# Wider entries in the token table of a routed expert layer: 64 bytes instead of 8, with the table filled later

## The reference, cut to what matters

```
x = x + tanh(g_xattn) * attention(layernorm(x), ctx, ctx)     # 8 heads, over the features
xt = layernorm(x).reshape(-1, 512)                             # 2048 tokens
probs = softmax(xt @ wg)                                       # 8 experts
idx = argmax(probs); gate = probs[idx]
out = gate * (xt @ W[idx].T + b[idx])                          # only the chosen expert counts
x = x + tanh(g_ffn) * out
```

## Time and profile before

| | us |
|---|---|
| three runs, median (lowest to highest) | 635.13 (632.38 to 635.82) |
| the profiled execution's own time | 634.65 |
| its span, first to last instruction | 633.0 |
| PE busy | 534.4 |
| DVE busy | 451.8 |
| POOL busy | 370.9 |
| ACT busy | 349.5 |

### The profile page before, as it was taken

The page is one execution under the profiler, slowest core; times in us unless marked ns, Lnnn a source line. Parts: engine busy times, 40 slices in busy tenths (PEclk is TensorE's granted clock), DMA queues, the critical chain, the costliest instruction groups (busy, mean ns, idle before and its releaser), DMA issues.

```text
span 633.0 us, 9589 instructions
## 1 busy us (share of the span) xinstructions
PE 534.4 (84%) x2603; PEld 181.2 (29%) x2603; DVE 451.8 (71%) x883; ACT 349.5 (55%) x429; POOL 370.9 (59%) x631
## 2 busy tenths in 40 slices
PE   0177999999999999999889999998699699199993
PEld 0011222323323233232223233232222145045551
DVE  5587799889898898989988898889686545001110
ACT  2221768677787777878657777865467521011110
POOL 6434458867675776768575777857253733424441
PEclk9999999999999999999989999999999799689997
DMA  4755375766667577665454657574720433323410
GB/s 128 200 141 175 71 185 137 194 164 194 181 185 220 157 186 181 181 181 131 127 152 101 156 140 136 135 128 96 67 86 1 153 130 118 111 82 108 130 52 0
DMA packets 35045, 85.52 MB, mean 135 GB/s; under 512 B 10232, under 2 KB 10364, under 8 KB 34976
## 3 DMA queue, kind: packets, MB, share of 16 engines
q1 hardware_dynamic: 22848, 59.46, 39.1%
q0 software_dynamic: 12160, 25.62, 12.2%
HBM read 62.56 MB, written 27.15 MB: 142 GB/s over the span
## 4 chain that ended last, share of the span: by engine, by line
PE 44%; DVE 29%; DMA 8%; issue 7%; ACT 4%; POOL 4%; SPq 1%; another core or an unknown queue 1%; POOLq 0%; ACTq 0%; DVEq 0%
DVE neg_max L801 21%; PE ps_scores L1223 11%; PE ps_pv L1166 11%; PE ps_ring L1129 11%; PE ps_scores L1147 6%; ACT probs L726 3%; DMA prep<-k_perm 2%; DMA table_dram<-entries,dest_i 1%; DMA stacks<-shift_parts 1%; DVE den_turned L827 1%; PE ps_scores L1206 1%; PE ps_pv L1175 1%; POOL prep L472 1%; PE ps_pv L1183 1%; DMA recs<-recs_dram,token_cols 1%
## 5 line engine op out<-in xcount | busy, mean ns | idle before, releaser
L801 DVE TENSOR_REDUCE neg_max<-ps_ring 128x1 f32<-128x512 f32 x512 | 333.3, 682 | 58.6 <-PE ps_ring L1129 51.4
L726 ACT ACTIVATE probs<-ps_scores 128x1024 f32<-128x1024 f32 x256 | 250.2, 1022 | 94.5 <-PE ps_scores L1147 86.7
L1129 PE MATMUL ps_ring<-stacks 96*128 96x512 bf16 x512 | 199.9, 404 | 58.9 <-DMA stacks<-parts_dram 29.5
L1147 PE MATMUL ps_scores<-stacks 128*128 128x512 bf16 x512 | 155.9, 387 | 9.4 <-ACT probs L726 5.5
L1166 PE MATMUL ps_pv<-probs,v_ones 128*32 128x512 f32 x1024 | 138.6, 614 | 0.0
L1129 PEld LDWEIGHTS ps_ring<-stacks 96*128 96x128 bf16 x512 | 49.5, 97 | 251.5 <-DVE neg_max L801 201.7
L1223 PE MATMUL ps_scores<-w_sb,f_xt 128*128 x184 | 84.9, 605 | 0.9 <-ACT f_xt L719 0.9
L1147 PEld LDWEIGHTS ps_scores<-stacks 128*128 128x128 bf16 x512 | 48.1, 101 | 54.6 <-ACT probs L726 18.2
L519 POOL DMA_DIRECT2D stacks<-shift_parts x96 | 49.6, 520 | 20.3 <-POOL shift_parts L512 17.5
L719 ACT COPY f_xt<-ps_scores 128x512 f32<-128x512 f32 x23 | 13.4, 587 | 86.5 <-PE ps_scores L1206 86.5
L1223 PEld LDWEIGHTS ps_scores<-w_sb,f_xt 128*128 128x128 f32 x184 | 35.6, 195 | 37.2 <-issue 36.3
(11 more groups left out here) (139 smaller groups left out, 481.1 us busy)
## 6 DMA issues: line engine op xcount, KB each, us to landing
parts_dram<-prep POOLq DMA_DIRECT2D x16, 768.0 KB
stacks<-parts_dram SPq DMA_DIRECT2D x64, 192.0 KB
stacks<-parts_dram SPq DMA_DIRECT2D x64, 128.0 KB
w_sb<-w_t SPq DMA_DIRECT2D x16, 512.0 KB, 8.7
recs_dram<-rec SPq DMA_DIRECT2D x16, 512.0 KB, 11.4
prep<-x_perm SPq DMA_DIRECT2D x16, 256.0 KB, 5.0
prep<-k_perm SPq DMA_DIRECT2D x16, 256.0 KB, 8.7
v_in<-v_t SPq DMA_DIRECT2D x16, 256.0 KB, 9.9
```

The source lines that it names most:

```text
L726: nc.scalar.activation(probs[:, k % 2, 2 * jp:2 * jp + 2], ps_scores[:, jp], ACT.Exp).then_inc(exp_done, 1)
L801: nc.vector.tensor_reduce(neg_max[:, g, j, c:c + 1], ps_ring[:, u.slot(n)], AX.X, ALU.max, negate=True).then_inc(ring_free, 1)
L1129: nc.tensor.matmul(ps_ring[:, u.slot(n + c)], q_stack[0:KS, B.p, g, j, c * 128:(c + 1) * 128], k_stack[0:KS, B.p, g, j], start=True, stop= ...
L1147: last = nc.tensor.matmul(ps_scores[:, jp, j % 2], k_stack[0:KA, B.p, g, j, c * 128:(c + 1) * 128], q_stack[0:KA, B.p, g, j], start=True, ...
```

## The change: entries of 16 int32, and a later, larger fill

An entry becomes WIDE = 16 int32 (64 bytes), of which the first two are used as before. `table_dram` grows from 16384 * 8 bytes (128 KB) to 16384 * 64 bytes (1 MB), `entries` from 128 bytes to 1 KB and `slot_tokens` from 256 bytes to 2 KB in each partition; a block of 32 entries is 2 KB instead of 256 bytes. The fill moves from SP's list before the rounds to the end of `emit` of batch 1, behind `load_values` of batch 3, and reads each row of `none_i` eight times. POOL gets a fifteenth constant that clears all of `entries`, its first setting of `slot_tokens` is eight times as long, and the later ones set the token numbers alone.

```diff
--- before.py
+++ after.py
@@ -37,6 +37,7 @@
 
 
 TILE, ENTRY = 128, 32
+WIDE = 16
 NSLOT = NT // TILE + NE - 1
 
 
@@ -139,7 +140,7 @@
 
         parts_dram = nc.dram_tensor("parts_dram", [NB, 2, NP, ROWS, DM], BF16, kind="Internal").ap()
         recs_dram = nc.dram_tensor("recs_dram", [NT, REC], F32, kind="Internal").ap()
-        table_dram = nc.dram_tensor("table_dram", [NE * CAP, 2], I32, kind="Internal").ap()
+        table_dram = nc.dram_tensor("table_dram", [NE * CAP, WIDE], I32, kind="Internal").ap()
         table_blocks = table_dram.rearrange("(k p) o -> k (p o)", p=ENTRY)
 
 
@@ -209,7 +210,7 @@
         place = sb("place", [128, NB, NE])
         dest_f = sb("dest_f", [128, NB])
         dest_i = sb("dest_i", [128, NB], I32)
-        entries = sb("entries", [128, NB, 2], I32)
+        entries = sb("entries", [128, NB, WIDE], I32)
         count = sb("count", [128, NE])
 
         recs = sb("recs", [128, NREC, REC])
@@ -230,7 +231,7 @@
         expert_cols = sb("expert_cols", [128, 32])
         slot_expert = sb("slot_expert", [128, len(PHASES), 32], I32)
         choose_bias = sb("choose_bias", [128, len(PHASES), 32], BF16)
-        slot_tokens = sb("slot_tokens", [128, 32, 2], I32)
+        slot_tokens = sb("slot_tokens", [128, ENTRY, WIDE], I32)
         token_cols = sb("token_cols", [128, len(PHASES), 32], I32)
         gate_cols = sb("gate_cols", [128, len(PHASES), 32])
 
@@ -286,7 +287,7 @@
         STACK_CONSTS, VALUE_CONSTS = 2, 3
         DVE_CONSTS = 20
         BIAS_CLEAR = VALUE_CONSTS + 7
-        POOL_CONSTS = 14
+        POOL_CONSTS = 15
         block = ctx.enter_context(nc.Block())
 
         start_turns = Turns(0)
@@ -380,8 +381,6 @@
             load_rows_keys(Batch(1, 0))
             for g in range(NG):
                 load_stack(Batch(0, 1), g)
-            sp.wait_ge(pool_const, POOL_CONSTS)
-            sp.dma_start(table_dram.rearrange("(k p) o -> k (p o)", p=128), none_i[:]).then_inc(table_set, 16)
             sp.wait_ge(dve_const, BIAS_CLEAR)
             for j in range(3):
                 sp.dma_start(bias_rows[32 * j:32 * j + NE], bias.rearrange("(e n) -> e n", e=NE)).then_inc(bias_in, 16)
@@ -402,6 +401,10 @@
                 if stack:
                     load_stack(B.plus(2), 1)
                     load_values(B.plus(2))
+                if B.known(1):
+                    sp.wait_ge(pool_const, POOL_CONSTS)
+                    sp.dma_start(table_dram.rearrange("(k h p) o -> k h (p o)", h=WIDE // 2, p=256 // WIDE),
+                                 none_i[:].unsqueeze(1).to_broadcast([128, WIDE // 2, 256])).then_inc(table_set, 16)
 
             rounds(sp, emit)
             store_record(Batch(7, 0))
@@ -427,8 +430,10 @@
                                             allow_small_or_imprecise_dtypes=True),
                      lambda: nc.gpsimd.iota(slot_iota[:], [[0, 1]], base=0, channel_multiplier=1,
                                             allow_small_or_imprecise_dtypes=True),
+                     lambda: nc.gpsimd.iota(entries[:].rearrange("p b o -> p (b o)"), [[0, NB * WIDE]], base=0,
+                                            channel_multiplier=0),
                      lambda: nc.gpsimd.iota(entries[:, :, 0], [[ROWS, NB]], base=0, channel_multiplier=1),
-                     lambda: nc.gpsimd.iota(slot_tokens[:].rearrange("p q o -> p (q o)"), [[0, 64]], base=NONE,
+                     lambda: nc.gpsimd.iota(slot_tokens[:].rearrange("p q o -> p (q o)"), [[0, ENTRY * WIDE]], base=NONE,
                                             channel_multiplier=0),
                      lambda: nc.gpsimd.iota(count[:], [[CAP, NE]], base=0, channel_multiplier=0,
                                             allow_small_or_imprecise_dtypes=True)]
@@ -541,8 +546,7 @@
                 pool.wait_ge(table_out, 16 * GROUPS[PHASES[phase][0]][1])
                 if phase > 0:
                     pool.wait_ge(cols_ready, phase)
-                    chain.add(nc.gpsimd.iota(slot_tokens[:].rearrange("p q o -> p (q o)"), [[0, 64]], base=NONE,
-                                             channel_multiplier=0))
+                    chain.add(nc.gpsimd.iota(slot_tokens[:, :, 0], [[0, ENTRY]], base=NONE, channel_multiplier=0))
                     chain.settle()
                 pool.indirect_dma_start(slot_tokens[:].rearrange("p q o -> p (q o)"), None, table_blocks,
                                         bass.IndirectOffsetOnAxis(ap=slot_block[:, 0:1], axis=0),
```

## The result

Seven runs of the changed kernel gave a median of 630.1 us (628.8 to 631.65), seven of the kernel before 635.82 us (632.38 to 637.71). The ratio is 0.9914, with an interval from 0.9889 to 0.9939: the change makes the kernel faster by 0.6 to 1.1%. The profiled execution after took 630.53 us, 628.9 of them in the span, 4.1 less than the 633.0 before. Two executions far outside the others, one of 890.85 us in d1 and one of 1762.04 us in f1, are left out of the medians further down.

The account below looks back on a forecast made before the run. It took the chain as mostly PE and DVE, transfers counting only where an engine on it waits. Terms 0 - 0.2 + 0 + 0 + 0.35 - 0.05 = +0.1 us gave 635.2 us, range 632.3 to 638.3.

Parts of the forecast that it names:

- The scatters: 16 table scatters on POOL, each moving 8 KB instead of 1, said to be off the path: 0 us.
- The faster one: Rival: the old fill held up the stretch after 40 us; PE's whole 2.49 us wait goes, 632.9 us; chance 0.08.
- The term of the old fill: Removing the fill before the rounds shortens PE's wait ahead of batch 0's scores: gain of 0.2 us, between 0 and 2.49.
- The new fill: 1 MB fill on SP's queue at about 114 us, taking 3.0 us, hidden by idle engines and later room: 0 us.
- the rival of a dear fill: The moved fill is dear per packet, 7.0 us, and stalls batch 3 by 4.0 us: 639.2 us; chance 0.10.
- POOL's constants: Longer clearing and first setting at POOL's start, 0.78 us, covered by 0.91 us of idle time: 0 us.
- The reads: Table reads: the earlier ones hidden; the last, on the chain, +0.35 us (0 to 1.94), its clearing 0.05 off.
- The third rival: Wide blocks slow at the end: last read of 4.4 us and doubled transposes, 1.94 + 0.45, so 637.2 us; chance 0.08.

Follow-up runs that it names:

- d1: The changed kernel plus twelve extra scatters of packed 8-byte entries to an unread scratch tensor, at the places of the kernel before: 636.77 us, ratio 1.0017.
- f1: The kernel before with an unread 8 KB tensor declared behind the table and filled once: 635.71 us, ratio 1.0013.
- e6: The kernel before, 8-byte entries and early fill, with 128 more entries per expert, so regions 17,408 bytes apart: 628.03 us, ratio 0.9894.
- f3: The kernel before without the scatters of batches 0 to 11: 627.25 us, but only the stretch ahead of 480 us is to be compared.
- f4: The kernel before with scatters of batches 0 to 11 sent by token number into one stretch: 629.35 us, only ahead of 480 us to be compared.
- a2: The changed kernel measured once more, unaltered: 629.42 us, ratio 0.9911.
- e2: The changed kernel with its 1 MB fill back in the old place before the rounds, so the width alone: 629.14 us, ratio 0.9909.
- e1: The changed kernel with entries of 8 bytes, so the moved fill alone: 637.02 us, ratio 1.0016.
- e3: The changed kernel, entries still 64 bytes apart, but scattering only the first 8 bytes of each: 629.67 us, ratio 0.9908.
- e4: The changed kernel with entries of 32 bytes: 630.45 us, ratio 0.9902.
- e5: The changed kernel with entries of 16 bytes, so regions 32,768 bytes apart: 629.35 us, ratio 0.9903.
- e7: The changed kernel with the weights of batch 0 loaded in batch 8: 627.67 us, ratio 0.9892.
- f6: The same kernel as e7, measured again: 630.15 us, ratio 0.9921.
- f5: The kernel before with the edits of e6 and e7 together: 627.93 us, ratio 0.9891.
- f2: The kernel before, 8-byte entries, with 4096 entries per expert, so regions 32,768 bytes apart: 628.73 us, ratio 0.9898.

## Why the prediction was wrong

- **The scatters: the step that failed.** "No gain, then, and no cost." The prediction asked who waits for a scatter's landing, found nobody, and stopped. It did not ask what a scatter does to other transfers. Shown by e6, f3 and f4: the eight groups of 8-byte entries 16,384 bytes apart hold up shift rows, values and record stores in batches 12 to 14, from some 4 us to 9 for the shift rows, even when they are issued 10 us behind the last scatter (442.2 and 451.9 us), and with that goes a batch 14 whose first half is 4.7 us longer. The worth was some 5.6 us of the rounds. The premise behind it, that a transfer counts only where an engine on the chain waits for it, missed a transfer that slows others.
- **It was to be seen in the trace of before.** The prediction compared shift rows with their reader in batches 2 and 15 alone, 5.0 to 5.4 us and 1.6 us. In batch 12 they took 9.4, in batch 14 8.4; a half batch took 18.29 us where 13.6 was possible; ACT stood 5.42 us without a named releaser; and 1% of the chain was "an unknown queue". None of this names the scatters, but they lie there.
- **None of the rivals had it.** The faster one was at the start, and went the other way: PE's wait there did not fall from 2.49 us but rose to 3.96 (3.17 in a2). Its first scores came at 59.44 us, not within 0.5 of 57.4. The term of the old fill, -0.2, had the wrong sign: the wait is 2.09 to 2.72 us in the profiles with the early fill (before, e2, e6, f1 to f4) and 3.07 to 3.96 with the moved one (after, a2, e1, e3, e4, e5). At the fourth turn the first seven stand at 86.14 to 87.02 us, the other six at 87.79 to 88.75, so the move itself cost some 1 to 2 us. (Of the kernels with extra scatters, d1 has the moved fill and a wait of 2.50 only.) With the fill early but eight times as long (e2) the wait is 2.09, SP's bias loads are held for 12.61 us and the weights go out behind them at 55.71. That fits the weights' traffic as the cause, and so do the shorter waits of e7, f6 and f5 (2.13, 2.45 and 1.80); in the whole time f6 does not bear it out.
- **The new fill held, by some luck.** 3.0 us assumed, 3.05 measured by its packets; no wait of PE or DVE on a DMA in batches 2 to 4; so the rival of a dear fill fell. The wait of 3.1 us estimated from the Trainium skill's figure did not come either. But the store that gave the price is less near than the prediction said: in its nine slices POOL's queue moved 183 packets and 0.70 MB, some 4 KB each where the fill's are 1 KB, and 0.09 of the 0.79 MB were SP's loads.
- **POOL's constants held.** 0.78 us under a cover of 0.91: the idle time shrank from 0.91 to 0.21 us and POOL came 0.08 us later, 0.78 in sum.
- **The reads.** The first was hidden, as said: POOL's shift rows behind it went out at 481.56 us, 2.87 ahead where PE was 3.84 ahead at the turn of 476.51, and their first reader on PE still came 3.84 ahead (485.62 against 489.46). The last was mis-sized: 2.46 to 3.35 us, 0.89 instead of 0.35, within its bounds of 0 to 1.94. The clearing stayed at 0.23, where 0.05 was taken off. The third rival's other half, dear transposes, did not come: 0.24 us.

By its two terms that came out as a loss (1.47 us at the start, 0.89 at the end) the change would have been slower; the unseen one was worth more than both.

**What stays open.** Why a step of 16,384 bytes is slow while 17,408 is not, and why 32,768 is half-way with 8-byte entries (8.6 and 5.3 us) and nearer to well with 16 (e5, 6.4 and 3.5); no run shows the inside of the memory. The Trainium skill ("DMA: Bandwidth & Descriptors", section "Latency and other measured facts") tells of plain copies that lose rate at row steps that are large powers of two (207 GB/s at 512 KiB, 164 at 2 MiB, 103 at 4 MiB), and of a few KiB more per row as the cure. The step here is 16 KiB, the writes are scattered, and 1 KiB was enough, so that rule is kin to it at most. Why the delay builds up, and why it outlasts the scatters: for the shift rows of 339 us, after the first two scatters, the least landing is alike (3.1 us before, 3.0 after); for those of 366 us it is 5.2 and 3.1, but 5.0 in e6 as well; only from 393 us on do before and e6 part. And which transfer released ACT and DVE at 456 us; both wait there only for PE by the program, and PE's ends are modelled. The stall comes and goes with the step of the regions (18.29 us before, 20.36 in e1, 19.25 in f1; 13.59 in e6, 13.60 in f2), but the link in between was not seen.

## What to carry to other kernels

Follow the landing time of one small, regular transfer through the whole run: where it doubles while the bytes on the engines fall, something else is slowing the engines, and no wait of its own will name it. Small packed writes scattered into regions whose distance is a power of two are a suspect (shown here for 16,384 bytes, in part for 32,768); lengthen the regions by a little before widening the entries. Here 128 entries of padding per expert (e6, 628.03 us) gave no less than a table eight times as large (629.42 beside it, with intervals that overlap), with no larger fill to hide and no larger read at the end.

## What was not expected of the hardware

- Eight groups of 8-byte writes 16,384 bytes apart, 128 writes in each scatter, slowed unrelated transfers to 72 GB/s over 10 us, with 33 to 131 GB/s in slices that were five to nine tenths busy; with 17,408 bytes the same stretch carried 152 GB/s (0.72 MB and 1.52 MB in 10 us).
- An indirect scatter costs POOL the same for 8 and for 64 bytes per partition: 988 ns and 986 ns in the median.
- The slowness outlasted the scatters: the last was issued at 442.2 us, and from 452 to 456 us a packet of SP's queue still took 1.0 us in the mean, against 0.13 after.
- A store of 1 MB from on-chip memory in packets of 1 KB took 47.7 ns a packet, 3.05 us of 16 engines (after).
- Two executions of the same kernel (e7 and f6) differ by 2.8 us behind the rounds, where the granted clock stood at 1.2 GHz after PE's standstill for some 4 us in one and some 13 us in the other.
